# A branch hint at the head of the main loop of four engines, in a decoder layer on one core

## The reference

```python
x = layernorm(x + attn(x))        # 16 heads; only the 64 largest scores of each row are kept
x = layernorm(x + xattn(x, ctx))  # one-head cross attention
x = layernorm(x + ffn(x))         # a weighted sum of 8 chosen adapter matrices

# inside attn
scores = einsum('bhqd,bhkd->bhqk', qn, kn) / temp      # qn, kn: unit-length queries and keys
vals, idx = top_k(scores, 64)
out = einsum('bhqk,bhkd->bhqd', scatter(softmax(vals), idx), v)
return gate * (out @ Wo + bo) + (1 - gate) * x
```

## Time and profile before

| what | before |
|---|---|
| median of 3 runs | 3950.44 us (3947.05 to 3951.39) |
| the profiled execution | 3949.0 us, its span 3947.1 us |
| TensorE busy | 3015.7 us (76%) |
| VectorE busy | 2799.5 us (71%) |
| ScalarE busy | 2132.2 us (54%) |
| GpSimd busy | 1875.5 us (48%) |
| mean granted TensorE clock | 0.884 |

### The profile page before, as it was taken

The page is one execution under the profiler, slowest core; times in us unless marked ns, Lnnn a source line. Parts: engine busy times, 40 slices in busy tenths (PEclk is TensorE's granted clock), DMA queues, the critical chain, the costliest instruction groups (busy, mean ns, idle before and its releaser), DMA issues. The chain is left out here.

```text
span 3947.1 us, 59251 instructions
## 1 busy us (share of the span) xinstructions
PE 3015.7 (76%) x16154; PEld 1684.0 (43%) x16154; DVE 2799.5 (71%) x9325; ACT 2132.2 (54%) x5970; POOL 1875.5 (48%) x2307
## 2 busy tenths in 40 slices
PE   3687888887788778778877888888877887778855
PEld 2244444444444444444444444444443444444432
DVE  4467768776777777777777776877777777677772
ACT  1455555565555565555655555566555565555541
POOL 0345555453465444455444555454445544445423
PEclk7888899998889988889988889998898998889877
DMA  5000000000000000000000000000000000000000
GB/s 179 6 15 20 7 21 21 15 21 20 18 10 20 15 20 21 20 7 20 20 15 20 21 12 16 20 15 21 20 21 7 20 21 15 20 17 15 10 9 11
DMA packets 43387, 80.95 MB, mean 21 GB/s; under 512 B 3692, under 2 KB 11884, under 8 KB 42758
## 3 DMA queue, kind: packets, MB, share of 16 engines
q1 hardware_dynamic: 41254, 68.75, 5.1%
q0 software_dynamic: 1504, 5.77, 0.4%
HBM read 57.73 MB, written 16.78 MB: 19 GB/s over the span
## 5 line engine op out<-in xcount | busy, mean ns | idle before, releaser
L476 POOL TENSOR_SCALAR probs<-probs,kept_inv 128x256 f32<-128x256 f32 x1024 | 639.3, 642 | 1231.6 <-DVE kept_inv L1661 1231.6
L1632 DVE SCALAR_TENSOR_TENSOR probs<-scores,threshold,probs 128x256 f32<-128x256 f32 x1007 | 451.6, 505 | 369.6 <-issue 369.2
L741 ACT ACTIVATE near<-scores 128x256 f32<-128x256 f32 x1024 | 413.9, 428 | 160.0 <-DVE nearest L1602 160.0
L721 ACT ACTIVATE scores<-score_ps,neg_guess 128x256 f32<-128x256 f32 x1024 | 398.9, 492 | 146.2 <-DVE kept_inv L1661 87.0
L1598 DVE MATCH_REPLACE8 near<-nearest,near 128x256 f32<-128x256 f32 x1024 | 406.6, 406 | 0.0
L979 PE MATMUL work_ps<-ident,probs 128*128 128x128 f32 x2072 | 341.9, 308 | 53.3 <-POOL probs L476 25.2
L449 POOL TENSOR_TENSOR inv_norm<-sumsq,minus_half 128x32 f32<-128x32 f32 x64 | 373.3, 5833 | 5.3
L1594 DVE MAX8 nearest<-near 128x8 f32<-128x256 f32 x1024 | 356.8, 409 | 0.3
L1602 DVE MAX8 nearest<-near 128x8 f32<-128x256 f32 x1024 | 356.8, 409 | 0.0
L756 ACT ACTIVATE probsT<-work_ps 128x512 f32<-128x512 f32 x512 | 291.6, 599 | 106.3 <-PE work_ps L1144 75.1
L1675 DVE SCALAR_TENSOR_TENSOR rows<-gate_t,rows 128x512 f32<-128x512 f32 x64 | 51.8, 810 | 404.3 <-POOL rows L497 404.3
(11 more groups left out here) (167 smaller groups left out, 5756.8 us busy)
## 6 DMA issues: line engine op xcount, KB each, us to landing
x_in<-in_x_dram SPq DMA_DIRECT2D x32, 512.0 KB, 3.5
x_res<-in_x_dram SPq DMA_DIRECT2D x32, 512.0 KB, 4.4
out_dram<-rows SPq DMA_DIRECT2D x32, 512.0 KB, 3.0
c_sb<-in_ctx_dram SPq DMA_DIRECT2D x32, 256.0 KB, 2.8
scores<-in_L_ffn_W_dram SPq DMA_DIRECT2D x4, 1024.0 KB, 5.3
near<-in_L_ffn_W_dram SPq DMA_DIRECT2D x4, 1024.0 KB, 5.3
w_q<-in_L_attn_Wq_dram POOLq DMA_DIRECT2D x1, 1024.0 KB, 10.7
probs<-in_L_xattn_Wq_dram SPq DMA_DIRECT2D x1, 1024.0 KB, 9.9
```

The lines of the kernel that those rows point to most:

```text
L476: pool.tensor_scalar(probs[:, s % 2, h, j], probs[:, s % 2, h, j], kept_inv[:, s % 2, n:n + 1], 1.0, ALU.mult, ALU.mult).then_inc(s_pr, 1)
L721: last = act.activation(scores[:, s % 2, h, j], score_ps[:, j, h], ACT.Identity, bias=neg_guess[:, t, n:n + 1])
L741: last = act.activation(near[:, h, j], scores[:, s % 2, h, j], ACT.Sign, accum_out=sign_sum[:, s % 2, n:n + 1])
L1632: step.mark(dve.scalar_tensor_tensor(out=probs[:, r, h, j], in0=scores[:, r, h, j], scalar=threshold[:, r, k:k + 1], in1=probs[:, r, h, j] ...
```

## The change

The four loops are opened by another call, which does the same and also places one branch hint as the first instruction of each turn. The hint names the loop's closing branch as one that will be taken. Nothing else differs.

```diff
@@ gpsimd
-            with pool.Fori(1, B // 2 - 1) as k:
+            with nc.Fori(1, B // 2 - 1, engines=[pool.engine], hint_back_edge=True) as k:
@@ scalar
-            with act.Fori(1, B // 2 - 1) as k:
+            with nc.Fori(1, B // 2 - 1, engines=[act.engine], hint_back_edge=True) as k:
@@ tensor
-            with pe.Fori(1, B // 2 - 1) as k:
+            with nc.Fori(1, B // 2 - 1, engines=[pe.engine], hint_back_edge=True) as k:
@@ vector
-            with dve.Fori(1, B // 2 - 1) as k:
+            with nc.Fori(1, B // 2 - 1, engines=[dve.engine], hint_back_edge=True) as k:
                 body(k * 2, 0, "steady")
                 body(k * 2 + 1, 1, "steady")
                 step.restart()
```

## The result

The changed kernel takes 3980.03 us (median of 4 runs, 3976.55 to 3984.0) against 3948.74 us of the kernel before on the same chip (4 runs, 3946.17 to 3951.39). The ratio is 1.0079, with a 95% interval of 1.0066 to 1.0091: 31.3 us slower. Slower was the likelier sign of the prediction, but the size is three times that of its sum (+9.5), and the time lies outside its range. The profiled execution took 3976.55 us, its span is 3974.7 us, and the granted clock was 0.874 (0.884 before).

A forecast was written before the change was run, and what follows sets the result against it. VectorE's largest idle time was waiting for GpSimd, then issue stalls behind keep_top's far jumps. 0 (jumps back) + 0 (hints) + 9.5 (shift) took the profiled 3949.0 to 3958.5, 3960 as median; 8 in 10: 3948 to 3967.

The forecast's parts named there:

- The hints themselves: Cost of the hint instruction on each engine, once a turn: 0 to 2.7 us, taken as 0 because waits cover it.
- One place further on: VectorE's later code moves one place (the shift), delaying two keep_top places by about 0.4 us: 10.4 us, taken as 9.5.
- The jumps back: Stalls at the loops' 13 jumps back vanish but become waits for other engines: -0.9 to +6.0 us, taken as 0.
- (a): Rival: all VectorE and ScalarE jump-back stalls come back as time, 69.6 us less, 3890 with the shift; 3 in 100.
- (b): Rival: VectorE's hint lost to eight far jumps before its branch, ScalarE's acts: 3954.5 us; 15 in 100.
- (c): No shift cost, as loader aligns code or a GpSimd wait absorbs 0.4 us: 3949.5 to 3956.5, likeliest 3951; 17 in 100.
- (d): Hint's fetch delays a far jump's piece: one keep_top per turn waits 2.4 us, 3993; on GpSimd 3964; together 13 in 100.

The follow-up runs named there:

- experiment 4: Changed kernel, all four hints, with VectorE's loop loaded one place earlier so its code stands where it stood before the change: 3972.46 us, ratio 1.0061.
- experiment 2: Changed kernel without VectorE's hint; ScalarE, TensorE and GpSimd keep theirs: 3946.06 us, ratio 0.9992 to the kernel before.
- experiment 5: Changed kernel with VectorE's hint moved behind the last keep_top of the turn, ahead of mixing: 3946.51 us, ratio 0.9991 to the kernel before.
- experiment 3: Kernel before, no hint, with one empty instruction added at the head of VectorE's turn: 3950.56 us, ratio 1.0008.
- experiment 1: Kernel before with the hint on VectorE's loop alone: 3986.08 us, ratio 1.0091.
- kernel 8: Changed kernel, VectorE's jump-back hint replaced by one per keep_top far jump, each landing moved to place 62 of a fetched piece: 3907.96 us, ratio 0.9892.

## Why the prediction was wrong

**The step that failed is "The hints themselves".** It priced the instruction, put its upper bound at one short GpSimd instruction, 2.7 us for 14 turns, and took 0 because each hint stands ahead of a wait. The instruction itself does cost next to nothing, 50 ns on VectorE by its row. What the step left out is what happens between a hint and its branch. With the hint at the head of the turn the branches of VectorE's keep_tops in the turn are dearer (medians 63 to 133 and 56 to 116 ns), and 8 keep_tops stand in the turn. That is 19 us in the 14 rare keep_tops and 8 us in the 98 common ones, by experiment 4, where the shift is taken out and 24 us of time are lost. Experiments 2 and 5 take it away in two ways, without a hint and with one that has no keep_top behind it, and both are at 3946 us. The mean granted clock of TensorE was lower wherever the loss was (0.874 in the change, 0.877 in experiment 4, 0.884 before), and TensorE was busy 13.5 us longer in the change; no run separates this from the longer keep_tops, whose growth is as large as the loss without it.

**The rare path was left out of the sum.** I used batches 2 and 4, "neither takes the rare path", and counted it only as places that the shift loses. It is taken in 14 of 112 keep_tops of the loop, but has ten or eleven compare-and-branches at a time. So it carries 70% of the growth under the hint.

**One place further on** was right in its mechanism and about right in its size. The fourth L1632 starts late itself, at 791.11 where the end of the piece now stands, the sixth at 859.98; the two places are 0.41 and 0.36 us longer in the change, 13 times each. The change has 9.3 us more of common keep_top than experiment 4, against 10.4 forecast, and the two places are the only ones. (Behind the fourth L1632 four follow, not the five that the prediction has; the term doesn't hang on it.) As time it is 7.6 us by the medians of the change and experiment 4, and 2.5 us alone (experiment 3); the term of 9.5 was too big, and by how much is not settled. The rows of the changed kernel at batch 5, step 3:

```profile
789.58 0.48 DVE L1632 SCALAR_TENSOR_TENSOR probs<-scores,threshold,probs 128x256 f32<-128x256 f32 x1
...
791.11 1.04 DVE L1632 SCALAR_TENSOR_TENSOR probs<-scores,threshold,probs 128x256 f32<-128x256 f32 x1 [1.03 <-issue]
```

**The jumps back** came out as worked out from the first turn: both stalls gone, L487 at 1.23 us, the second choose_sides waiting 2.80 us for ScalarE, ScalarE's copy 0.42 us earlier, L490 1.47 us later. The value of 0 is borne out for VectorE: experiment 1 lost 38.0 us where its keep_tops alone grew by 36.0. It is borne out for TensorE, whose stall of 3.3 to 3.8 us, unseen by me, was covered. The other three hints together gain some 2 us (experiment 2), at most 7; that this is ScalarE's share I only argue, from the 0.42 us that I had seen (5.5 for 13) and let the rest of the chain use up.

**The rivals.** (a) fell: the stalls went and no time came. (b) fell too: the stall of VectorE's jump back went, although eight far jumps lie between the hint and its branch. The Trainium skill, "Runtime: NRT & Kernel Launch", section "Instruction fetch mechanics", which spoke for (b), has prefetch purely sequential. Here the trace differs: at step 3 of kernel 8 the fetch 2.1 us ahead of the jump brought the target, and the one at 1.0 us behind it was no longer made. (c) fell in its first form, since the two landings moved. Its second form, the 0.4 us absorbed in a wait, is open: alone the shift cost 5.1 us of keep_top and 2.5 us of time, with none inside the interval. (d), the hint in the way, with 3993 us, was nearest in sign and size, but not in kind: it had one keep_top in a turn wait for another fetch of 2.4 us. The trace shows fewer fetches and no such single wait; the price is spread over all branches. The sum by what was measured: 19.1 (rare) + 8.3 (common) + 9.3 (shift) = 36.7 us of keep_top, less 2 to 6 for the other three hints, is 31 to 35 us, against 31.3. It counts every microsecond of keep_top as time, which experiment 4 (27.5 us for 24) nearly does and experiment 3 (5.1 for 2.5) can't tell.

## What to carry to other kernels

A hint is not priced by its own row but by the branches between it and its target: count them, those of the rare paths most of all, and place the hint behind the last one, but so that a fetched piece still ends between it and its jump; a trace of the stall shows whether it acts. The stall at VectorE's jump back ended in a wait for another engine and was worth nothing as time, and the loop's first turn, which is entered without a jump, had shown this before anything was changed. The stalls worth removing here were not those of the loop's branch but those of the eight jumps over rare code in each turn.

## What the runs showed of the hardware

- While its branch hint was pending, VectorE's other compare-and-branches took longer: medians 63 to 133 ns and 56 to 116 ns, and 0.16 to 0.23 us more idle time around a test and its jump. The hint itself took 44 to 61 ns.
- A hint acted where one of the fetched pieces of 128 instructions ended between it and its jump (six places of kernel 8, down to 6 instructions between that end and the jump) and did nothing where both were in one piece (two places of kernel 8, 45 instructions apart, and experiment 5, 13 instructions and 17.8 us apart). The fetch at the piece's end then brought the jump's target.
- A far jump that a hint serves leaves 4.56 us of keep_top where it was 6.88. A hint that acted for a jump that was then not taken made the rare keep_top 2.2 us longer.
- TensorE's branch back took 3.3 to 3.8 us without a hint and 0.34 to 0.39 us with one, in the record of the branch itself. With its hint, the queue q8 has 144 packets of 16.4 KB in place of 156; the other instruction queue, q14, moves 8.2 KB at a time.
- One instruction more at a loop's head cost 0.2 to 0.4 us at two landings in eight, through the ends of fetched pieces alone.
